# A decoder layer with mixture of experts: q and k of the self attention produced with features on the partitions

## What is computed

```python
q, k, v = heads(h @ Wq + bq), heads(h @ Wk + bk), heads(h @ Wv + bv)   # 16 heads of 16
q, k = rope3d(q), rope3d(k)        # 3 parts of 4 features: frame, row, column of the token
x = x + softmax(q k^T / 4) v @ Wo + bo                     # self attention
x = x + cross_attention(ln(x), ctx, mask) @ W_fc.T         # q = ln(x), k = v = ctx, / 16
x = x + top2_of_8_experts(ln(x))                           # 256 -> 1024 -> 256, exact gelu
```

## Time and profile before

| | us |
|---|---|
| median of 3 runs | 703.58 (701.61 to 703.88) |
| the profiled execution | 703.05 |
| its span, first to last instruction | 701.3 |
| TensorE busy | 659.6 |
| VectorE busy | 491.0 |
| ScalarE busy | 427.7 |
| GpSimd busy | 275.1 |

### The profile page before, as it was taken

The page is one execution under the profiler, slowest core; times in us unless marked ns, Lnnn a source line. Parts: engine busy times, 40 slices in busy tenths (PEclk is TensorE's granted clock), DMA queues, the critical chain, the costliest instruction groups (busy, mean ns, idle before and its releaser), DMA issues.

```text
span 701.3 us, 16282 instructions
## 1 busy us (share of the span) xinstructions
PE 659.6 (94%) x5043; PEld 471.9 (67%) x5043; DVE 491.0 (70%) x1339; ACT 427.7 (61%) x789; POOL 275.1 (39%) x581
## 2 busy tenths in 40 slices
PE   8888899999999999999978999999999999999996
PEld 4555576666766666666654579889898955554795
DVE  2397787685876887858873425437887788999881
ACT  4444657567575778767644677656556545566751
POOL 4233325354234445543274163632232323333342
PEclk9999999999999999999998999999999999999999
DMA  5535445454555454775496451432131253445222
GB/s 137 151 107 151 138 136 154 146 159 138 138 157 173 125 168 132 208 205 155 129 321 229 167 208 47 117 76 40 32 48 33 41 129 93 103 104 103 45 28 23
DMA packets 55229, 87.52 MB, mean 125 GB/s; under 512 B 9821, under 2 KB 43497, under 8 KB 54121
## 3 DMA queue, kind: packets, MB, share of 16 engines
q1 hardware_dynamic: 45097, 74.23, 36.5%
q0 software_dynamic: 7600, 9.90, 8.6%
q10 hardware_dynamic: 2448, 2.36, 1.0%
HBM read 60.15 MB, written 25.97 MB: 123 GB/s over the span
## 4 chain that ended last, share of the span: by engine, by line
PE 60%; DVE 15%; issue 8%; SPq 7%; ACT 4%; POOL 4%; DVEq 1%; DMA 1%; another core or an unknown queue 0%; ACTq 0%; POOLq 0%
PE attention_psum L856 11%; PE attention_psum L863 9%; PE attention_psum L848 7%; DVE over L1575 5%; PE attention_psum L798 5%; PE attention_psum L817 5%; PE attention_psum L919 4%; PE attention_psum L742 3%; PE attention_psum L753 3%; PE attention_psum L747 3%; SPq L646 3%; PE attention_psum L883 3%; PE attention_psum L872 3%; DVE neg_max L1478 2%; ACT weights L1094 1%
## 5 line engine op out<-in xcount | busy, mean ns | idle before, releaser
L1478 DVE TENSOR_REDUCE neg_max<-attention_psum 128x2 f32<-128x512 f32 x256 | 165.2, 682 | 36.4 <-PE attention_psum L798 36.1
L1080 ACT ACTIVATE weights<-attention_psum 128x512 f32<-128x512 f32 x256 | 147.2, 594 | 67.8 <-PE attention_psum L817 52.4
L1575 DVE STREAM_TRANSPOSE over<-over 32x64 f32<-32x64 f32 x448 | 105.6, 236 | 6.1
L798 PE MATMUL attention_psum<-weights 99*128 99x256 bf16 x512 | 98.7, 275 | 9.1 <-DVE neg_max L1478 7.9
L817 PE MATMUL attention_psum<-weights 102*128 102x256 bf16 (+1 forms) x512 | 102.4, 273 | 4.2 <-issue 1.5
L1200 ACT ACTIVATE weights<-attention_psum,b_sb 128x128 f32<-128x128 f32 x200 | 57.2, 370 | 59.7 <-PE attention_psum L856 54.1
L856 PE MATMUL attention_psum<-over,v 128*128 128x128 f32 x736 | 88.0, 276 | 3.3 <-issue 2.1
L863 PE MATMUL attention_psum<-weights 128*128 x400 | 90.8, 380 | 0.2
L856 PEld LDWEIGHTS attention_psum<-over,v 128*128 128x128 f32 x736 | 85.3, 192 | 7.1 <-DVE over L1575 3.5
L1827 POOL DMA_INDIRECT out<-over x25 | 42.0, 1681 | 113.1 <-DVE over L1592 103.8
L1836 POOL TENSOR_TENSOR weights<-weights 128x512 bf16<-128x512 f32 x32 | 37.0, 1158 | 114.2 <-ACT weights L1239 114.0
(11 more groups left out here) (221 smaller groups left out, 1142.2 us busy)
## 6 DMA issues: line engine op xcount, KB each, us to landing
parts<-weights SPq DMA_DIRECT2D x96, 128.0 KB
weights<-parts SPq DMA_DIRECT2D x64, 192.0 KB
weights<-parts SPq DMA_DIRECT2D x64, 128.0 KB
weights<-in_L_ffn_w SPq DMA_DIRECT2D x8, 1024.0 KB
loose<-in_L_ffn_b SPq DMA_DIRECT2D x22, 256.0 KB
weights<-parts SPq DMA_DIRECT2D x64, 64.0 KB
w_sb<-in_L_ffn_w SPq DMA_DIRECT2D x8, 512.0 KB
weights<-in_L_ffn_w SPq DMA_DIRECT2D x8, 512.0 KB
```

The lines of the kernel that those rows point to most:

```text
L798: last = pe.matmul(bank[:, t * S:(t + 1) * S], q[0:MAX0, h % HALF, t * P:(t + 1) * P], k[0:MAX0, h % HALF, :], start=True, stop=True)
L1080: act.activation(m.p[:, u % P_RING, :], m.b_bank[u % B_RING], ACT.Exp, scale=SCALE[ORDER[u // H][0]]).then_inc(m.b_free[u % B_RING], 1)
L1478: v.tensor_reduce(m.neg_max[:, :, h:h + 1], m.a_bank[u % A_RING].rearrange("p (t k) -> p t k", t=T), AXX, ALU.max, negate=True).then_inc(m ...
L1575: last = v.transpose(m.xT[n % 2][q:q + QUAD, :, r:r + QUAD], x[r:r + QUAD, :, q:q + QUAD])
```

## The change

q and k of the self units are made with features on the partitions. Per unit and w (q or k), `qk_a` and `qk` now make the even and the odd features: 128 weight columns at a step of two stand, and the 256 turned tokens pass. A partition then holds a feature pair's even member in the first half of a row of 512 and its odd member in the second. VectorE makes the rotation from PSUM: `qk` adds the bias and multiplies with the cosine (two fused operations of 256), `rope` does it for the partner with the sine into `swapped` (two more) and frees the bank, `roped` adds (512 elements). The `stack` pieces of self units no longer use TensorE or a bank of the ring, and the fillers of the first go with them; ScalarE casts from SBUF, `rest` reads SBUF. `write` stores each part of a self unit with two DMAs of 512 bytes a row in place of one of 1 KB. Heads of self units lie in natural order, so `values` and `ot` lose a permutation there.

The table of cosines and sines is a load of 128 rows of 4 KB (16 copies of 8 rows, 512 KB) in place of 16 KB, and lies where the last expert's first weights come later, whose load now waits for the last rotation. The biases of q and k are loads of 8 bytes a partition in place of 1 KB.

Pieces have new places in `SELF_AT`, `CROSS_AT`, `BOTH_AT`, `AFTER_SELF`, `AFTER_CROSS` and `AFTER`; `FIRST_AT`, `SECOND_AT`, `LAST_AT` and `WARM` stay.

```diff
@@ -95,26 +95,25 @@
...
     inv = np.float32(1.0) / np.float32(10000.0) ** (np.arange(2, dtype=np.float32) / np.float32(2.0))
-    cos, sin = [], []
-    for at in (position // 16, position % 16):
+    cos, sin = np.ones((HD, S), np.float32), np.zeros((HD, S), np.float32)
+    for first, at in ((4, position // 16), (8, position % 16)):
         freq = at.astype(np.float32)[:, None] * inv
-        cos += [np.cos(freq), np.cos(freq)]
-        s = np.concatenate([np.sin(freq), np.sin(freq)], axis=1)
-        s[:, 0::2] *= -1
-        sin.append(s)
-    return np.concatenate(cos + sin, axis=1).astype(np.float32)
-
-
-
-SELF_AT = ((-38, "x"), (-33, "ln_a", 0), (-30, "ln_d", 0), (-29, "turn"), (-27, "qk_a", 0), (-26, "qk", 0), (-25, "rope",
-        0), (-24, "qk_a", 1), (-23, "qk", 1), (-21, "rope", 1), (-21, "roped", 0), (-21, "roped", 1), (-20, "v",
-        0), (-15, "v", 1))
-CROSS_AT = ((-38, "cx"), (-32, "ln_a", 1), (-26, "keys"), (-22, "ln_d", 1), (-16, "vcross"))
-
-BOTH_AT = ((-19, "stack", 0), (-19, "rest", 0), (-18, "mid", 0), (-18, "write", 0), (-17, "stack", 1), (-17, "rest", 1),
-        (-16, "mid", 1), (-16, "write", 1), (-9, "read", 0, 0), (-8, "read", 0, 1), (-7, "read", 1, 0), (-4,
-        "read", 1, 1), (11, "max", 0), (11, "max_parts", 0), (11, "max_rows", 0), (15, "max_parts", 1), (17,
-        "max", 1), (20, "max_rows", 1))
+        for d in range(4):
+            cos[first + d] = np.cos(freq)[:, d % 2]
+            sin[first + d] = np.sin(freq)[:, d % 2] * (-1 if d % 2 == 0 else 1)
+    return np.stack([t.reshape(HD // 2, 2, S) for t in (cos, sin)], axis=1).reshape(HD // 2, 4 * S)
+
+
+
+SELF_AT = ((-38, "x"), (-33, "ln_a", 0), (-31, "ln_d", 0), (-29, "turn"), (-27, "qk_a", 0), (-27, "v", 0), (-25,
+        "qk", 0), (-25, "rope", 0), (-23, "qk_a", 1), (-22, "qk", 1), (-21, "rope", 1), (-21, "roped", 0), (-21,
+        "roped", 1), (-17, "v", 1))
+CROSS_AT = ((-34, "cx"), (-31, "ln_a", 1), (-26, "keys"), (-23, "ln_d", 1), (-12, "vcross"))
+
+BOTH_AT = ((-19, "stack", 0), (-19, "rest", 0), (-18, "mid", 0), (-18, "write", 0), (-18, "stack", 1), (-17, "rest",
+        1), (-16, "mid", 1), (-13, "write", 1), (-9, "read", 0, 0), (-8, "read", 1, 0), (-7, "read", 0, 1), (-4,
+        "read", 1, 1), (9, "max_parts", 0), (12, "max", 0), (13, "max_rows", 0), (15, "max_parts", 1), (17, "max",
+        1), (20, "max_rows", 1))
...
@@ -155,8 +154,8 @@
...
         "top", 10, 0), (3, "low", 12, 0), (3, "top", 12, 0), (2, "low", 13, 1))
-AFTER_SELF = ((19, "xbias"),)
-AFTER_CROSS = ((31, "ln_a", 2), (33, "store"), (36, "ln_d", 2), (37, "rturn"), (39, "logits"))
+AFTER_SELF = ((20, "xbias"),)
+AFTER_CROSS = ((28, "store"), (33, "ln_a", 2), (35, "ln_d", 2), (37, "rturn"), (39, "logits"))
...
@@ -167,7 +166,8 @@
...
 LISTED_AT = ((43, 2), (44, 2), (44, 0))
-AFTER = ((9, "o_move", 0), (17, "o_move", 1), (19, "ot", 0), (21, "ot", 1), (23, "cturn"), (26, "proj_a"), (27, "proj"))
+AFTER = ((10, "o_move", 0), (17, "o_move", 1), (19, "ot", 0), (20, "ot", 1), (23, "cturn"), (27, "proj_a"), (27,
+        "proj"))
...
@@ -314,7 +314,7 @@
...
         rung = [p for s in self.slots for p in s.pieces
-                if p[0] in RING and not (p[0] == "xturn" and p[2] >= SQUARES)]
+                if p[0] in RING and p[:2] != ("stack", SELF) and not (p[0] == "xturn" and p[2] >= SQUARES)]
...
@@ -376,7 +376,7 @@
...
         self.wqkv = under([P, KC, 3 * D])
-        self.qk = under([P, 2, T, D])
+        self.qk = under([P, 2, KC * S])
...
@@ -399,16 +399,15 @@
...
         self.r_bias = sba("r_bias", [P, E + L])
-        self.bias_qkv = first([P, 3 * D])
+        self.bias_v, self.bias_qk = first([P, D]), first([P, 2, 2])
         self.bias_o = first([P, D])
-        self.table = first([P, T, 2, 8])
+        self.table = self.w1_sb0[:, E - 1, :].rearrange("p (w x s) -> p w x s", w=2, x=2)
...
         self.neg = sba("neg", [32, PARTS, P], BF16)
-        self.turn_a = first([P, 2, T, H, 8])
-        self.turn_b = first([P, 2, T, H, 8])
+        self.swapped = first([P, 2, KC * S])
...
@@ -551,6 +551,10 @@
...
+    def written(self, i):
+
+        return sum(16 * PARTS * (2 if a == SELF else 1) for a, n in ORDER[:i + 1])
+
...
@@ -571,10 +575,11 @@
...
                      w.rearrange("(c p) n -> p c n", p=P)).then_inc((m.s_wq, m.s_wk, m.s_wv)[i], 16)
-    for i, b in enumerate((bq, bk, bv)):
-        sp.dma_start(m.bias_qkv[:, i * D:(i + 1) * D],
-                     b.rearrange("(a d) -> a d", a=1).broadcast_to([P, D])).then_inc(m.s_qkv, 16)
-    sp.dma_start(m.table[:, :, :, :], rope.rearrange("(t p) (a d) -> p t a d", p=P, a=2)).then_inc(m.s_qkv, 16)
+    for i, b in enumerate((bq, bk)):
+        sp.dma_start(m.bias_qk[:, i, :], b.rearrange("(p x) -> p x", x=2)).then_inc(m.s_qkv, 16)
+    sp.dma_start(m.bias_v, bv.rearrange("(a d) -> a d", a=1).broadcast_to([P, D])).then_inc(m.s_qkv, 16)
+    sp.dma_start(m.w1_sb0[:, E - 1, :],
+                 rope.rearrange("(a d) x -> a d x", a=1).broadcast_to([H, HD // 2, 4 * S])).then_inc(m.s_qkv, 16)
...
@@ -623,8 +630,14 @@
...
                     sp.wait_ge(made, i + 1)
-                    sp.dma_start(parts[i, w, part].rearrange("d h s -> h d s"),
-                                 m.parts[w][:, part, :]).then_inc(m.s_write[w], 16)
+                    if a == CROSS:
+                        sp.dma_start(parts[i, w, part].rearrange("d h s -> h d s"),
+                                     m.parts[w][:, part, :]).then_inc(m.s_write[w], 16)
+                    else:
+                        for x in range(2):
+                            sp.dma_start(parts[i, w, part, x * HD // 2:(x + 1) * HD // 2].rearrange(
+                                "d h (c s) -> (h c) d s", c=KC), m.parts[w][:, part, x * S:(x + 1) * S]
+                                ).then_inc(m.s_write[w], 16)
...
@@ -633,7 +646,7 @@
...
                     sp.wait_ge(m.s_fixed, i + 1)
-                sp.wait_ge(m.s_write[w], 16 * PARTS * (i + 1))
+                sp.wait_ge(m.s_write[w], m.written(i))
...
@@ -845,7 +859,7 @@
...
                     pe.wait_ge(m.b_free[u % B_RING], u // B_RING + 1)
-                last = pe.matmul(m.o_bank[32 * j:32 * j + 32, g * S:(g + 1) * S], v[:, t, head_at(h), :],
+                last = pe.matmul(m.o_bank[32 * j:32 * j + 32, g * S:(g + 1) * S], v[:, t, head_at(h) if a else h, :],
...
@@ -905,18 +919,17 @@
...
             elif name in ("qk_a", "qk"):
-                t = piece[3]
+                w = piece[3]
                 if name == "qk_a":
-                    if (n, t) == (0, 0):
-                        pe.wait_ge(m.s_wq, 16)
+                    if n == 0:
+                        pe.wait_ge((m.s_wq, m.s_wk)[w], 16)
                     pe.wait_ge(*m.emptied(("turn", a, n)))
-                    bank = fill(("qk", a, n, t))
-                elif (n, t) == (0, 0):
-                    pe.wait_ge(m.s_wk, 16)
-                w = 0 if name == "qk_a" else 1
-                bank = m.bank_of(("qk", a, n, t))
+                    bank = fill(("qk", a, n, w))
+                odd = 0 if name == "qk_a" else 1
+                bank = m.bank_of(("qk", a, n, w))
                 for c in range(KC):
-                    last = pe.matmul(bank[:, w * D:(w + 1) * D], m.xnT[:, c, t, :], m.wqkv[:, c, w * D:(w + 1) * D],
+                    last = pe.matmul(bank[:, odd * S:(odd + 1) * S], m.wqkv[:, c, w * D + odd:(w + 1) * D:2],
+                                     m.xnT[:, c, :, :].rearrange("p t q -> p (t q)"),
...
@@ -929,13 +942,10 @@
...
                 last.then_inc(m.fills(piece), 1)
-            elif name == "stack":
+            elif name == "stack" and a == CROSS:
...
                 bank = fill(piece)
-                if a == SELF:
-                    pe.wait_ge(m.s_roped, 2 * n + w + 1)
-                    turn_rows(piece, bank, m.qk[:, w])
-                elif w == 0:
+                if w == 0:
...
@@ -1229,13 +1239,19 @@
...
                 w = piece[3]
-                act.wait_ge(*m.filled(piece))
+                if a == SELF:
+                    act.wait_ge(m.s_roped, 2 * n + w + 1)
+                else:
+                    act.wait_ge(*m.filled(piece))
                 if i > 0:
-                    act.wait_ge(m.s_write[w], 16 * PARTS * i)
-                act.copy(m.parts[w][:, 0, :], m.bank_of(piece)).then_inc(m.s_hi[w], 1)
+                    act.wait_ge(m.s_write[w], m.written(i - 1))
+                act.copy(m.parts[w][:, 0, :], m.qk[:, w, :] if a == SELF else m.bank_of(piece)).then_inc(m.s_hi[w], 1)
...
                 w = piece[3]
-                act.wait_ge(*m.emptied(("stack", a, n, w)))
+                if a == SELF:
+                    act.wait_ge(m.s_rest[w], n + 1)
+                else:
+                    act.wait_ge(*m.emptied(("stack", a, n, w)))
...
@@ -1489,15 +1505,18 @@
...
             elif name == "qk":
-                t = piece[3]
-                if (n, t) == (0, 0):
+                w = piece[3]
```

(48 more changed lines are left out.)

20 lines of the change are left out of this document (14 added, 6 removed).

## The result

The median went from 703.73 us (four runs) to 711.13 us (four runs, 709.48 to 712.77): a ratio of 1.0086, 95% interval 1.0059 to 1.0113. The change made the kernel 0.86% slower; 699.0 with a range of 694 to 706 was forecast. The profiled execution of after took 711.15 us around a span of 709.3.

A forecast was written before the change was run, and what follows sets the result against it. TensorE's instruction list was taken to set the pace after 66 us, VectorE's order from 44 to 66, a latency chain before 36. Terms -4.4 + 0.9 - 0.7 = -4.2 us gave 699.0 us, range 694 to 706.

The forecast's parts named there:

- The clock: Start, before 36 us: TensorE's idle pattern and low-clock cost stay nearly as before; 0, bounds -1.7 and +1.7 us.
- Theory A: Forecast for e1: filling the idle time ahead of two turns removes the low clock behind them, 4 to 6 us less.
- rival (3): Before 62 us: TensorE idles longer, each further stretch at 1.2 GHz costs 1.7 to 2 us; 702.8 with two; 12%.
- VectorE: Self units: +0.48 us of work each, hidden under TensorE from 66 us on; +0.9 us where VectorE bounds.
- rival (1): Units 3 to 7: VectorE becomes the bound, having no idle time left before its maxima; +2.6, 705.7 us; 7%.
- The fused operation: VectorE's bias and product on 256 elements, priced as a plain operation at 0.33 us; doubled, +2.6 us a unit.
- TensorE, what goes: Self units lose two stack pieces of 0.44 us each; counted in units 3 to 7 only, -4.4 us.
- TensorE, what is altered: q and k projections: loading weights at a step of two costs 0 extra, hidden while below 220 ns.
- Rival (2): q and k projections: the weight load with a step doubles, +20.5 us, 719.4 us; 4%.
- The start: Chain from the first projections to unit 1's layer norm becomes 0.7 us shorter, with the larger table in time; -0.7 us.
- rival (4): Start: the table of cosines and sines lands at 16 to 18 us; 701 to 702.6 us; 8%.
- Sync queue and places: Self units' doubled write issues and the moved pieces: taken as 0, bounds -6 to +6 us.

The follow-up runs named there:

- e7: The kernel before with the new places from the sixth unit in order on and the old ones ahead of it; 701.30 us, ratio 0.9978.
- e1: The changed kernel with 11 more fillers ahead of each of two turns, those of units 2 and 3; 706.57 us, ratio 1.0046.
- e6: e1 with plain products for the fused operations, leaving out the biases of q and k; 704.27 us, ratio 1.0014.
- e5: e1 with four fillers of 512 columns ahead of the second v of units 3 to 7; 709.10 us, ratio 1.0075.
- e9: e1 with the two sums of a self unit apart, the first three steps earlier, the second one later; 703.73 us, ratio 0.9991.
- e3: The kernel before with the new places and nothing else; 704.44 us, ratio 1.0016.
- e2: The changed kernel with the places of before; 723.38 us, ratio 1.0281.
- e12: The changed kernel with the two sums of a self unit apart and no filler added; 707.73 us, ratio 1.0043.
- e11: e10 with the maxima rows of the third unit from the end stored seven and two steps earlier; 701.94 us, ratio 0.9975.
- e10: e9 with one DMA a part in the writes of self units; 702.29 us, ratio 0.9976.

## Why the prediction was wrong

**The clock: this step failed.** The prediction said of the start "That is nearly the old pattern, so I take the same cost", with 0 in the sum and 1.7 us as its upper bound. It looked for gaps before 36 us only. There the pattern was indeed the old one (in after idle 2.00 us ahead of the second `v`, then 1.65 and 0.73, close to the 1.5 and 2 forecast). The gaps that cost are at 38 and 65 us, in the stretch where "others bind" and where removing TensorE work was put down as free. It wasn't at 38 us: that work had kept TensorE busy while the chain of unit 2's layer norm ran. e7, which has before's code there, has 0.28 us of idle time ahead of that `turn` where after has 2.47. Of the difference the two transposes are 0.9 us. The other half is that ScalarE's normalisation started 1.15 us later (39.56 against 38.41), behind a later start of VectorE's moments (34.81 against 34.48) and GpSimd's eight operations, which took 3.6 us instead of 2.8. That stretch was worth 3.6 to 3.9 us at step 8. The gap at 65 us is not of the change's making, since e7 has 2.38 us there. Theory A was rival (3) in substance. Its price of 1.7 to 2 us a stretch was about right, as the two stretches behind the `turn` gaps cost 2.8 to 3.7 us together by the fillers that took them away; its chance of 12% was too small, and its 702.8 too low because it stood on the sum of -4.2 us. The rule of the Trainium skill that went with it (TensorE: Matmul & The Clock Gate, Part 1; the throttled state is the default and activity releases it) agrees with e1, where idle time filled with unread work turned 0.53 into 1.00.

**VectorE: the order was left out.** The prediction counted VectorE's work (+0.9 us in the stretch it bounds, hidden behind 44 us of idle time from 66 us on) and not how it is cut. The spread sums are worth 3.0 to 3.9 us at equal work. VectorE is busy 75.5% from 66 to 242 us, so rival (1), which needed it to have no idle time, is not what happened; an engine three quarters busy holds up another when 2.0 us of its list stand in one piece and the other has two banks of scores ahead.

**The fused operation.** "I price the fused operation as a plain one of its size" is off by 60 ns, 0.40 us start to start instead of 0.33. By e6 that is 2.2 us of the result.

**TensorE, what goes.** -4.4 us was right in kind and too large: with 4.3 us put back e5 is 2.0 us slower by its ratio (not clear of noise), 3.2 from step 24 to 168. In after none of it is seen as such, for from step 24 to 168 the changed kernel gains 2.8 us and the new places alone, in e7, 2.7. With the sums apart (e9) it is 6.0, of which some may have been lost before and taken back, as e3 and e7 suggest for the places. The period of a self and a cross unit, forecast at 42.6 us, is 43.3 in after (L931 of SELF 6 and 7 in its timeline) and 42.7 in e9:

```profile
181.43 1.14 PE L931 MATMUL attention_psum<-weights 128*128 128x256 f32 x4
...
224.72 0.49 PE L931 MATMUL attention_psum<-weights 128*128 128x256 f32 x1
```

```profile
173.89 1.14 PE L931 MATMUL attention_psum<-weights 128*128 128x256 f32 x4
...
216.59 1.14 PE L931 MATMUL attention_psum<-weights 128*128 128x256 f32 x4
```

**TensorE, what is altered: right.** The load at a step of two lasts 197 ns (190 before) and stays under 220. Rival (2) is out. Line 931 of after (ns min/median/max):

```profile
L931 PEld LDWEIGHTS attention_psum<-weights x128: 193/197/338, 11.3 to 233.4; 128*128 128x128 f32 x128
```

By the Trainium skill (SBUF — State Buffer, Door 1: The DMA port swizzle) a step up to four fp32 elements runs at full rate; the trace is 4% off that.

**The start: 0.3 us of the 0.7.** The first score came 1.5 us earlier (34.23 against 35.76), but in e7 (34.44) and e3 (34.97), which start with the code of before, it came 1.3 and 0.8 us earlier too. What differs is whether the clock fell at 28 us: 16 projection records took 5.41 us in before, 3.72 in e3 and e7, 3.73 in after. The layer norm's end, `turn` of unit 1, came at 27.11 against 26.96. Counted from the first projection, where the chain begins, it came after 15.82 us (11.29 to 27.11) against 16.14 in before (10.82 to 26.96), e3 and e7 alike: 0.3 us shorter. In e6, with plain products, it is 15.47, which is the 0.7 forecast, so what the term missed is the price of the fused operation. That the clock did not fall at 28 us, in after and in every other rotated kernel, was put at 0 and is luck as far as is shown. The first fused operation started at 13.39 instead of 12.90, released by TensorE, so the table was in time and rival (4) is out.

**Sync queue and places.** 0 was taken for both. Alone, the places are worth +0.16% (-0.07 to +0.39), which agrees. They are not neutral in the rotated kernel, though, where the old ones cost 12 us and more (e2), a dependence that the prediction had no term for. The doubled writes put the load of x 2.9 us later, and taking them out changed nothing that can be told.

**What stays open.** After loses 3.0 us between steps 224 and 255, with TensorE idle for 2.22 us at 338.7 ahead of L831 and the clock at 0.50 behind it; e1 and e9 lose 0.7 and 0.2 there, e12 2.9, and e11, aimed at the rows that L831 waits for, did not settle it. e10 has nearly the same wait (2.19 us, up to 333.5) and no fall behind it. Also left in every rotated kernel are 2.7 to 3.2 us at step 24 when fillers and order are mended; e6, which has no spread sums, has 2.2. And neither the fillers ahead of the `turn` of unit 3 nor the spread sums were tried on the kernel before. (The chances that the prediction adds up for "faster" make 62%, not 61; nothing rests on it.)
